# Graph attention with residual and layer norm: two blocks computed in turns, the order of the first loads, and who waits for the last stores

## What is computed

```
s_i = x @ attn[:d];  s_j = x @ attn[d:]
e = leaky_relu(s_i + s_j.T, negative_slope=0.2)
e = e + where(adj > 0, 0.0, -1e9)
alpha = softmax(e, axis=1)
out = layernorm(x + alpha @ x)        # eps 1e-5, no scale or shift
```

## Time and profile before

| | |
|---|---|
| median of 3 runs | 256.71 us (256.52 to 256.77) |
| the profiled execution | 257.18 us, span 255.3 us (1.9 us lie outside the span) |
| mean granted TensorE clock | 0.994 of full speed |
| TensorE matmul busy | 242.9 us, 95% of the span |
| VectorE busy | 233.6 us, 91% |
| ScalarE busy | 175.4 us, 69% |
| GpSimd busy | 36.5 us, 14% |
| bytes | 69.2 MB read, 2.1 MB written; 347 to 350 GB/s in most slices up to 80% of the span |

### The profile page before, as it was taken

How to read it: one execution, slowest core, us unless ns; L and a number is a source line. 1 busy time by engine, 2 the same in 40 slices (tenths; PEclk the granted TensorE clock), 3 DMA queues, 4 the chain that set the end, 5 groups by cost and what they waited for, 6 DMA issues and landing times.

```text
span 255.3 us, 2776 instructions
## 1 busy us (share of the span) xinstructions
PE 242.9 (95%) x801; PEld 127.9 (50%) x801; DVE 233.6 (91%) x383; ACT 175.4 (69%) x257; POOL 36.5 (14%) x76
## 2 busy tenths in 40 slices
PE   7998989989999999999999999999999999999980
PEld 6743434434444444444444444444444444899970
DVE  1979899989999999999999999999999999999552
ACT  0589999998499669495986579578965579204410
POOL 1000000000052003300430003300320004303322
PEclk9999999999999999999999999999999999999997
DMA  7999999999999999999999999999999940100101
GB/s 199 309 347 348 348 349 347 349 342 348 347 328 360 349 348 348 348 335 348 348 347 364 347 348 348 353 349 348 349 360 350 346 116 0 45 0 4 41 0 45
DMA packets 70227, 71.51 MB, mean 280 GB/s; under 512 B 2881, under 2 KB 68674, under 8 KB 70210
## 3 DMA queue, kind: packets, MB, share of 16 engines
q10 hardware_dynamic: 34592, 34.67, 43.5%
q1 hardware_dynamic: 34594, 34.67, 43.4%
q0 software_dynamic: 1024, 1.97, 2.5%
HBM read 69.21 MB, written 2.10 MB: 279 GB/s over the span
## 4 chain that ended last, share of the span: by engine, by line
PE 81%; ACT 6%; DMA 5%; issue 2%; ACTq 2%; SPq 1%; POOL 1%; DVE 1%
PE psum L866 69%; PE psum L870 11%; DMA adj_in<-in_adj_dram 5%; ACT xj L400 2%; ACTq L271 2%; ACT mask_bytes L412 2%; ACT mask_bytes L418 1%; PE psum L862 1%; SPq L253 1%; POOL out_dram L279 1%; ACT x_raw L503 0%; SPq L271 0%; DVE weights L721 0%; DVE x_raw L666 0%; SPq L292 0%
## 5 line engine op out<-in xcount | busy, mean ns | idle before, releaser
L866 PE MATMUL psum<-weights,xj 128*128 128x512 f32 x448 | 194.5, 593 | 2.9 <-ACT xj L400 2.0
L721 DVE SCALAR_TENSOR_TENSOR weights<-q_row,r_j,mask_t 128x512 f32<-128x512 f32 x256 | 172.2, 740 | 0.3
L866 PEld LDWEIGHTS psum<-weights,xj 128*128 128x128 f32 x448 | 84.0, 190 | 109.2 <-issue 82.2
L418 ACT ACTIVATE mask_bytes<-adj_in 128x4096 uint8<-128x4096 int32 x27 | 97.3, 3613 | 22.7 <-DMA adj_in<-in_adj_dram 15.2
L607 DVE STREAM_TRANSPOSE mask_t<-mask_bytes 128x1024 uint32<-128x1024 uint32 x27 | 33.4, 1236 | 0.9 <-ACT mask_bytes L418 0.9
L870 PEld LDWEIGHTS psum<-xj,weights 128*128 128x128 f32 x256 | 28.8, 192 | 0.5 <-issue 0.5
L870 PE MATMUL psum<-xj,weights 128*128 128x128 f32 x256 | 28.9, 275 | 0.0
L337 POOL TENSOR_SCALAR neg_mean<-total 128x4 f32<-128x4 f32 x7 | 1.6, 223 | 158.4 <-ACT x_raw L431 158.4
L431 ACT ACTIVATE x_raw<-x_raw 128x128 f32<-128x128 f32 x28 | 8.2, 295 | 15.3 <-DVE x_raw L666 15.3
L346 POOL DMA_DIRECT2D out_dram<-x_raw x28 | 14.6, 525 | 19.3 <-ACT x_raw L445 19.3
L412 ACT ACTIVATE mask_bytes<-adj_in 128x2048 uint8<-128x2048 int32 x9 | 17.0, 1901 | 0.0
(11 more groups left out here) (65 smaller groups left out, 81.7 us busy)
## 6 DMA issues: line engine op xcount, KB each, us to landing
adj_in<-in_adj_dram ACTq DMA_DIRECT2D x64, 512.0 KB, 13.0
adj_in<-in_adj_dram SPq DMA_DIRECT2D x64, 512.0 KB, 13.6
out_dram<-x_raw POOLq DMA_DIRECT2D x28, 64.0 KB, 5.3
x_raw<-in_x_dram ACTq DMA_DIRECT2D x4, 128.0 KB, 3.2
x_raw<-in_x_dram SPq DMA_DIRECT2D x4, 128.0 KB, 3.5
x_raw<-in_x_dram ACTq DMA_DIRECT2D x2, 256.0 KB, 6.1
x_raw<-in_x_dram SPq DMA_DIRECT2D x2, 256.0 KB, 7.0
out_dram<-x_raw POOLq DMA_DIRECT2D x4, 32.0 KB, 1.8
```

Source lines behind the costliest of these rows:

```text
L418: nc.scalar.activation(mask_bytes[:, g % BYTE_SLOTS, :, :, :], adj_in[:, g % ADJ_SLOTS, :, :, :], ACT.Sign).then_inc(bytes_ready, 1)
L721: nc.vector.scalar_tensor_tensor(weights[:, slot_of(n, c), :], q_row[:, n * BANK:(n + 1) * BANK], r_j[:, c:c + 1], mask_t[:, (n * PIECES + ...
L866: nc.tensor.matmul(banks[SUM_BANK[n % 2]][:, :], xj[:, c, :], weights[:, slot_of(n, c), :], start=(c == 0), stop=(c == CHUNKS - 1)).then_i ...
```

## The change

1. The pieces of blocks 0 and 1 are taken in turns. A list `ORDER` gives block and piece of each g: (0,0) (1,0) (0,1) (1,1) (0,2) (1,2) (0,3) (1,3), then block 2 and on as before. `END[n]` is the first g after block n's last piece: 7, 8, 12, ... All engines index by g and j (chunk within the piece). `scale_xj` now does 4 chunks per piece for g = 1 to 6 (behind both halves' bytes), where it did 8 for g = 1 to 3. `q_piece(1)` moves from g = 3 to ahead of piece 1's bytes. `take_sums(0)` moves from g = 4 to g = 7, `turn_back(0)` from g = 4 to g = 7, `residual(0)` from g = 6 to g = 9; those of block 1 stay at g = 9, 8 and 10.
2. Of the first half of piece 0, VectorE makes only two of the four rows k to bytes; ScalarE makes the others, ahead of `q_piece(0)`.
3. The last column of `xj` is a GpSimd copy of `d_j` instead of a third exponential on ScalarE.
4. SP issues its share of x's first part ahead of the attention row.
5. The 4 stores of the early group are split: GpSimd issues two, SP the other two, and SP waits for all of them. GpSimd doesn't wait for its stores any more.

```diff
+    ORDER = [(n, p) for p in range(PIECES) for n in range(2)] + [(n, p) for n in range(2, BLOCKS) for p in range(PIECES)]
+    END = [max(g for g in range(ALL_PIECES) if ORDER[g][0] == n) + 1 for n in range(BLOCKS)]
+    BY_DVE_TILES = 2
-    TAKE_SUMS_AT = [4, 9, 13, 18, 22, 27, 31]
+    TAKE_SUMS_AT = [7, 9, 13, 18, 22, 27, 31]
...
         @block.sync
+            load_x(sp, LOW_HALF, 0)
             sp.dma_start(attn_row_in[:], attn[:, :].rearrange("d o -> o d")).then_inc(attn_loaded, 16)
-            for part in range(X_PARTS):
+            for part in range(1, X_PARTS):
                 load_x(sp, LOW_HALF, part)
             for g in range(ALL_PIECES):
                 load_piece(sp, LOW_HALF, g)
+            for g in range(EARLY):
+                sp.wait_ge(early_out_ready, g + 1)
+                for q in LOW_HALF:
+                    store_last(sp, g, q, last_stored)
...
-            sp.wait_ge(last_stored, 16 * Q * (len(FINAL_GROUPS) - EARLY))
+            sp.wait_ge(early_stored, 16 * len(HIGH_HALF) * EARLY)
+            sp.wait_ge(last_stored, 16 * (Q * len(FINAL_GROUPS) - len(HIGH_HALF) * EARLY))
...
         @block.gpsimd
             nc.gpsimd.tensor_tensor(last_x[:], neg_last[:], d_j[:], ALU.mult).then_inc(last_x_ready, 1)
+            nc.gpsimd.tensor_copy(xj[:, :, DEN], d_j[:]).then_inc(xj_last_ready, 1)
...
                 pool.wait_ge(early_out_ready, g + 1)
-                for q in range(Q):
+                for q in HIGH_HALF:
                     store_last(pool, g, q, early_stored)
-            pool.wait_ge(early_stored, 16 * Q * EARLY)
...
         @block.scalar
-            nc.scalar.activation(xj[:, :, DEN], below_max[:], ACT.Exp, scale=SLOPE)
...
-                act.wait_ge(weights_used, (n + 1) * CHUNKS)
+                act.wait_ge(weights_used, END[n] * PC)
...
             act.wait_ge(max_scaled, 1)
+            act.wait_ge(adj_loaded[0], 16 * Q)
+            nc.scalar.activation(mask_bytes[:, 0, BY_DVE_TILES:K, :, 0:P], adj_in[:, 0, BY_DVE_TILES:K, :, 0:P],
+                                 ACT.Sign).then_inc(quarter_by_act_ready, 1)
             q_piece(0)
...
             scale_xj(3, PC)
+            q_piece(1)
             load_piece(act, HIGH_HALF[1:2], 3)
...
-                    if g < PIECES:
-                        scale_xj(g * PC, g * PC + K)
                     half_to_bytes(g, 1)
                     load_piece(act, HIGH_HALF[0:1], g + 3)
-                    if g < PIECES:
-                        scale_xj(g * PC + K, g * PC + PC)
...
-                if g == PIECES - 1:
-                    q_piece(1)
-                elif g >= PIECES and 2 * (g - PIECES) + 2 < RB:
+                if PC + (g - 1) * K < CHUNKS:
+                    scale_xj(PC + (g - 1) * K, PC + g * K)
+                if g >= PIECES and 2 * (g - PIECES) + 2 < RB:
                     q_piece(2 * (g - PIECES) + 2)
...
         @block.vector
-                nc.vector.tensor_scalar(mask_bytes[:, 0, :, :, part], adj_in[:, 0, :, :, part], 0.0, None,
-                                        ALU.is_gt).then_inc(half_bytes_ready, 1)
+                nc.vector.tensor_scalar(mask_bytes[:, 0, 0:BY_DVE_TILES, :, part], adj_in[:, 0, 0:BY_DVE_TILES, :, part], 0.0,
+                                        None, ALU.is_gt).then_inc(half_bytes_ready, 1)
                 dve.wait_ge(half_bytes_ready, 1)
+                dve.wait_ge(quarter_by_act_ready, 1)
                 turn_half(0, 0)
...
+            for g, (n, p) in enumerate(ORDER):
+                if p == 0:
+                    dve.wait_ge(q_ready, n + 1)
+                for j in range(PC):
...
+                    weigh(g, j)
+                    for m in range(BLOCKS - 1):
+                        if g * PC + j == END[m] * PC + RESIDUAL_AT:
+                            residual(m)
...
         @block.tensor
+            for g, (n, p) in enumerate(ORDER):
+                for j in range(PC):
+                    if n == 0:
+                        pe.wait_ge(xj_scaled, p * PC + j + 1)
+                        if g == 0 and j == 0:
+                            pe.wait_ge(xj_last_ready, 1)
+                    pe.wait_ge(weights_ready, g * PC + j + 1)
...
+                    for m in range(BLOCKS - 1):
+                        if g == END[m] and j == TURN_BACK_AT:
+                            turn_back(m)
```

More of the change, by code:

```diff
@@ L188, in gat_kernel @@
         last_x_ready = sem("last_x_ready")
+        xj_last_ready = sem("xj_last_ready")
+        quarter_by_act_ready = sem("quarter_by_act_ready")
         q_ready = sem("q_ready")
@@ L266, in load_piece @@
                 queue.wait_ge(half_bytes_ready, 1)
+                queue.wait_ge(quarter_by_act_ready, 1)
                 queue.wait_ge(first_bytes_ready, g - ADJ_SLOTS + 1)
@@ L281, in store_last, with slot_of @@
                             ).then_inc(done, 16)
-        def slot_of(n, c):
-            return (n * CHUNKS + c) % W_SLOTS
+        def slot_of(step):
+            return step % W_SLOTS
         block = ctx.enter_context(nc.Block())
@@ L715, in final_residual, with weigh @@
                         last_normalise(g - 1)
-            def weigh(n, c):
-                if n * CHUNKS + c >= W_SLOTS:
-                    dve.wait_ge(weights_used, n * CHUNKS + c - W_SLOTS + 1)
+            def weigh(g, j):
+                n, p = ORDER[g]
+                c = p * PC + j
+                if g * PC + j >= W_SLOTS:
+                    dve.wait_ge(weights_used, g * PC + j - W_SLOTS + 1)
                 nc.vector.scalar_tensor_tensor(
-                    weights[:, slot_of(n, c), :], q_row[:, n * BANK:(n + 1) * BANK], r_j[:, c:c + 1],
-                    mask_t[:, (n * PIECES + c // PC) % MASK_SLOTS, c // K % PF, :, c % K],
+                    weights[:, slot_of(g * PC + j), :], q_row[:, n * BANK:(n + 1) * BANK], r_j[:, c:c + 1],
+                    mask_t[:, g % MASK_SLOTS, j // K, :, j % K],
                     ALU.max, ALU.min).then_inc(weights_ready, 1)
-            for n in range(BLOCKS):
-                dve.wait_ge(q_ready, n + 1)
-                for c in range(CHUNKS):
-                    g = n * PIECES + c // PC
-                    if c % PC == 0 and g in HALVED:
+            for g, (n, p) in enumerate(ORDER):
+                if p == 0:
+                    dve.wait_ge(q_ready, n + 1)
+                for j in range(PC):
+                    if j == 0 and g in HALVED:
                         dve.wait_ge(half_mask_ready, HALVED.index(g) + 1)
-                    elif c % PC == 0 or c % PC == K and g in HALVED:
+                    elif j == 0 or j == K and g in HALVED:
                         dve.wait_ge(mask_ready, g + 1)
-                    weigh(n, c)
-                    if n > 0 and c == RESIDUAL_AT:
-                        residual(n - 1)
-                    if c % PC == SECOND_HALF_AT and g in HALVED:
+                    weigh(g, j)
+                    for m in range(BLOCKS - 1):
+                        if g * PC + j == END[m] * PC + RESIDUAL_AT:
+                            residual(m)
+                    if j == SECOND_HALF_AT and g in HALVED:
                         if g == 0:
@@ L743, in _ @@
                             turn_half(g, 1)
-                    if c % PC == (FIRST_TURN_AT if g == 0 else TURN_AT) and g + 1 < ALL_PIECES:
+                    if j == (FIRST_TURN_AT if g == 0 else TURN_AT) and g + 1 < ALL_PIECES:
                         if g + 1 < BY_DVE:
@@ L887, in _ @@
                     if n < BLOCKS - 1:
-                        block_product(n, c)
+                        block_product(g, j)
                     else:
                         for t in range(K):
-                            last = product(c, t)
+                            last = product(p * PC + j, t)
                         last.then_inc(weights_used, 1)
-                    if n > 0 and c == TURN_BACK_AT:
-                        turn_back(n - 1)
+                    for m in range(BLOCKS - 1):
+                        if g == END[m] and j == TURN_BACK_AT:
+                            turn_back(m)
             for t in range(K):
```

25 lines of the change are left out of this document (13 added, 12 removed).

## The result

The changed kernel takes 254.97 us (median; 254.04 to 255.84) against 256.71 us for the kernel before: ratio 0.994, 95% interval 0.9924 to 0.9955. That is 1.7 us won; the prediction said 254.9 us. The nine runs of the changed kernel spread over 1.8 us, the nine of the kernel before, measured together with them, over 0.6 us. The profiled execution is one of its longer ones: 255.71 us, span 253.9 us.

What follows compares the result with a forecast made beforehand. TensorE, busy 95% of the span, was taken as the bound, leaving the first product's start, its stalls and the end to win. End 1.8 us, turns and first bytes together nothing: 256.71 - 1.8 = 254.9 us, range 254.0 to 256.2.

Steps and rivals of the forecast that it cites:

- the prediction's own signs of being wrong: Whole kernel: GpSimd's drain still last, L810 starting after 5.8 us, or the last product moved by over 0.7 us.
- The end: Closing barrier: GpSimd, with two stores and no wait, drains from 249.8 to 252.5, ahead of SP; 1.8 us won.
- Rival 1: Closing barrier: the drain waits for landed stores, then takes 2.67 us; only 0.85 us won, 255.9 us; chance 0.12.
- Rival 2: Closing barrier: the drain ends at 255.1 wherever GpSimd begins it; nothing won, 256.7 us; chance 0.05.
- The first bytes: Piece 0 at the start: two engines finish at 18.53 instead of 18.71, first product near 20.2; 0.2 us won.
- The covering hole on ScalarE: ScalarE at piece 0: 1.20 us idle up to 19.37 takes the new instruction; otherwise 1.0 us lost.
- The attention row: SP's start queue: the row's issue moves back 0.9 us, but TensorE doesn't wait for it; 0 change.
- the bound of 5.8 us: Attention row's landing: up to 4.7 + 1.1 = 5.8 us a later row costs nothing, beyond it one for one.
- Rival 4: Start: attention row lands late behind x in SP's queue, one for one from 5.8 us; slower; chance 0.05.
- The turns: Blocks 0 and 1: stalls change place, 3.55 us against 3.35; costs 0.2, offset by the earlier first product.
- Rival 3: Blocks 0 and 1: smoother ScalarE load removes stalls at pieces 1 and 5, second residual covered; 1.5 us more, 253.4; chance 0.08.
- Rival 5: Blocks 0 and 1: stalls longer than computed, ScalarE's hole not taking the new instruction, 1.0; 255.9 us; chance 0.10.

Runs made afterwards that it cites:

- e12: The changed kernel measured again, unedited: 254.51 us, ratio 0.9927 to the kernel before.
- e1: Kernel before, but GpSimd issues two of the early group's four stores and waits for none, SP issues two and waits for all: 254.21 us, ratio 0.991.
- e5: The changed kernel, but GpSimd waits again for its two stores before the end: 255.36 us, ratio 0.9946 to the kernel before.
- e6: The changed kernel, but GpSimd issues all four early stores and waits for none, SP waits for all: 255.28 us, ratio 0.9946 to the kernel before.
- e3: The kernel before, with ScalarE making half of the first bytes of piece 0: 256.62 us, ratio 1.0008.
- e4: The changed kernel with the turns undone, on the piece order of before: 254.36 us, ratio 0.9932 to the kernel before.
- e7: The changed kernel with the attention row behind all three of SP's parts of x: 259.24 us, ratio 1.0116 to the kernel before.
- e8: The changed kernel with take_sums(0) behind piece 8's bytes (g = 8, not 7): 252.57 us, ratio 0.9836 to the kernel before.
- e10: e8 plus q_piece(1) behind the first half of piece 1's bytes and q_pieces 2 to 7 one piece later: 252.28 us, ratio 0.9835 to the kernel before.
- e11: e4 with take_sums(0) behind the next piece's bytes (g = 5 instead of 4): 253.28 us, ratio 0.9877 to the kernel before.
- e2: The kernel before with only the pieces of blocks 0 and 1 in turns and ScalarE's new order: 257.15 us, ratio 1.0036.

## Why the prediction was right, point by point

**The sum** came out, 254.9 forecast and 254.97 measured, but that it came out within 0.1 us is luck: the end gave 0.45 more than forecast, the first bytes 0.2 less, and the turns cost 0.5 to 0.7 in the first profile, nothing in the second (e12). One of the prediction's own signs of being wrong did appear: in the first profile the last product ended 0.87 us later than before, over its 0.7. In e12's it ended 0.49 us earlier. The other two signs, GpSimd's drain ending last and the first use of the attention row (L810, now L827) after 5.8 us, did not appear.

**The end: mechanism right, term too small.** 1.8 forecast, 2.25 measured from the mark in the profiles, 2.3 in e1's time. GpSimd's drain was expected from 249.8 to 252.5 and to be covered by SP's; it ran from 250.0 to 253.2 and was covered by 0.5 us. What I left out is that SP's side gets shorter too: from the mark to the end of SP's drain it is 5.5 us before and 5.1 after, although SP issues two stores more. With two stores on GpSimd SP's side is 5.1 us in e5 too, with four (e6) it is 5.5 again, so the last stores land sooner when GpSimd issues two. Rival 1 named a real cost at the wrong size: the drain is 3.25 us instead of 2.67 when it starts beside an issue, but it doesn't wait for the landing. Rival 2 is out: the end moved. The Trainium skill ("VectorE: DVE Perf Modes", "The DRAIN you can't avoid") gives about 12 ns for the drains of the runtime's preamble and postamble, on all five engines. The trace agrees for SP's drain in the closing barrier (7 ns in every run) and doesn't for GpSimd's (2511 to 3735 ns); that the page means this barrier's drains too is my reading. Had GpSimd's taken 12 ns in the kernel before, e1 could have won no more than the 0.4 us by which SP's side got shorter.

**The first bytes: wrong, small.** 0.2 forecast, 0 measured (e3). The step that failed took VectorE's and ScalarE's parts as starting together and the hand-over as free; a start 0.09 later and a hand-over of 0.09 ate it. Besides, in the changed kernel an earlier first product is lost again where ScalarE waits for piece 3 (the table at e12). The covering hole on ScalarE was right. In the changed kernel and in e4 the first product also starts 1.0 us after `weigh` 0 does, in the kernel before and in e3 0.85. The first two have TensorE's added wait for GpSimd's copy; whether that wait costs the 0.15 us was not tried.

**The attention row: right, its bound open.** L827 starts at 4.71 as before, and e7 confirms the price of a late row, about one for one. It doesn't confirm the bound of 5.8 us, which took VectorE's two idle times from one profile. Rival 4 was a real mechanism: in e6 the row held TensorE up by 0.2 us.

**The turns: each stall where it was put, sum too small by 0.5 to 0.7 in the first profile.** Forecast against the changed kernel's first profile: chunk 8, 0.7 and 0.64; from there to chunk 6 of piece 4, 0.65 and 1.16; behind `take_sums(0)`, 1.2 and 1.36; residuals 0.8 and 0.83. e12's profile gives 0.67, 0.4, 1.36 (with 1.26 for the stall itself, as in the first profile) and 0.83, a sum of 3.3 where I had 3.35. The failing term is the second: I took piece 4's landing from one profile (42.38) as a fixed number. ScalarE, relieved of half its `scale_xj`, runs into the landing of pieces 3 and 4, and piece 3's bytes start 15.3 to 16.4 us after the first product (e8 and the changed kernel). In the kernel before ScalarE was the later one and hid it. The two profiles of the changed kernel differ by 1.37 us in time and by 1.39 in the start of piece 3's bytes, so the landing is also where the spread of 1.8 us comes from, as far as these profiles show; a kernel that fixes the landing was not tried. Rival 3 (the turns pay) is true only with `take_sums(0)` moved, e8 and e10 against e11. Rival 5 (1.0 us more stalls) is near what e2 measured, 0.9, though not by the mechanism that it named: ScalarE's hole took the new instruction (e3).

**What I didn't see:** that the stalls are coupled. I added the stall behind `take_sums(0)` and the residuals' 0.8 us as two terms, though my own working set VectorE's lead to zero by the first to get the second. e8 takes away both with one move.

## What to carry to other kernels

Let the engine whose last act before the final barrier is slow arrive there early: give the waiting for the last stores, and as many of the stores as fit, to an engine that is quick to leave. When an engine's copy has to wait for a consumer, put what other engines need from it ahead of the wait, even if it is longer (3.6 us of bytes ahead of a 0.6 us copy won 1.9 us). A stall that empties a lead costs again at the next burst of work, so count leads along the whole chain and not stall by stall; and when a relieved engine begins to wait for a transfer, its time takes on the transfer's spread.

The fastest kernels here are e8 and e10, 252.57 and 252.28 us, 0.9836 and 0.9835 of the kernel before: the whole change with `take_sums(0)` behind piece 8's bytes.

## What the runs showed of the hardware that I had not expected

- GpSimd's drain at the end takes 2.67 us (kernel before) or 2.51 (e5) when its stores have landed, and 3.22 (e8) to 3.74 (e6) when it starts during its own store issues; it ended 2.57 us after the last of them in the changed kernel and 2.94 in e6. What it does in that time no run shows.
- Stores of 16 KB from SP and ScalarE land later while four stores of 32 KB go out through GpSimd: medians of 1.9 and 2.1 us in the kernel before and 1.8 and 2.0 in e6, against 1.7 and 1.8 us in the changed kernel, with two.
- A load of 1 KB behind 1 MB of x in the same queue was there 6.2 us after its issue (e7); behind the first part of x alone, issued at 1.63 us, it was there by 4.7 (changed kernel).
